# How the experts of a two-layer mixture-of-experts tower get their rows: scattered by expert, or gathered by a table from slot to token

## The reference, cut to what matters

```python
# layer 0, experts (xe: the layer-normed rows that go to expert e)
for e in range(N_EXPERTS):
    mask = (max_ind == e)[:, None]
    xe = jnp.where(mask, x, 0.0)
    oe = jax.nn.silu(xe @ w1[e]) * (xe @ w2[e]) @ w3[e]
    out = out + jnp.where(mask, oe, 0.0)
out = out.astype(jnp.bfloat16) * max_prob
# layer 1, experts
selection = scores + expert_bias[None, :]
_, top_idx = jax.lax.top_k(selection, K)             # K = 2
top_s = jnp.take_along_axis(scores, top_idx, axis=-1)
comb = jnp.zeros((T, e)).at[jnp.arange(T)[:, None], top_idx].add(top_s / (sum of top_s))
out = routed + _swiglu(xf, sg, su, sd)               # routed: sum over e of comb[:, e] * swiglu_e(xf)
```

## Time and profile before

| | us |
|---|---|
| median of 3 runs (1969.52 to 1982.78) | 1977.91 |
| the profiled execution itself | 1965.71 |
| its span | 1964.1 |
| PE busy in the span | 1599.7 (81%) |
| DVE, ACT, POOL busy | 1080.7, 619.3, 385.6 |
| mean granted TensorE clock (1 is full speed) | 0.884 |
| layer 0: last of `route` on DVE, first pair on PE | 842.64, 890.44 |
| layer 1: first shared pair, first routed pair, first pair of the tail | 1439.86, 1571.02, 1843.41 |

### The profile page before, as it was taken

The page is one execution under the profiler, slowest core; times in us unless marked ns, Lnnn a source line. Parts: engine busy times, 40 slices in busy tenths (PEclk is TensorE's granted clock), DMA queues, the critical chain, the costliest instruction groups (busy, mean ns, idle before and its releaser), DMA issues. The chain is left out here.

```text
span 1964.1 us, 28517 instructions
## 1 busy us (share of the span) xinstructions
PE 1599.7 (81%) x8996; PEld 873.7 (44%) x8997; DVE 1080.7 (55%) x2460; ACT 619.3 (32%) x840; POOL 385.6 (20%) x442
## 2 busy tenths in 40 slices
PE   5769998998999997608999479988632899999973
PEld 3412332332333325605666246677621566666642
DVE  5868996997998924612333355545620233333345
ACT  3403665665666683101111111101100122222110
POOL 6530000000000001151110460001157011111255
PEclk9856998998999998758999689997666899999987
DMA  3487222222222006011111210005012011111123
GB/s 90 126 145 223 36 33 33 33 33 33 33 33 33 1 2 187 9 59 42 40 40 36 71 28 2 2 1 166 1 50 76 7 48 52 52 52 52 50 81 91
DMA packets 86416, 106.98 MB, mean 54 GB/s; under 512 B 10481, under 2 KB 72244, under 8 KB 85300
## 3 DMA queue, kind: packets, MB, share of 16 engines
q1 hardware_dynamic: 74624, 82.39, 17.4%
q0 software_dynamic: 10752, 22.03, 3.8%
q10 hardware_dynamic: 960, 1.57, 0.5%
HBM read 61.82 MB, written 44.14 MB: 54 GB/s over the span
## 5 line engine op out<-in xcount | busy, mean ns | idle before, releaser
L510 DVE TENSOR_REDUCE sa_half_max<-psum 128x1 f32<-128x512 f32 x768 | 494.5, 687 | 65.6 <-PE psum L614 45.9
L568 ACT ACTIVATE sa_probs<-psum 128x1024 f32<-128x1024 f32 x384 | 372.6, 1022 | 169.2 <-PE psum L605 167.6
L614 PE MATMUL psum<-k_stack,q_stack 96*128 96x512 bf16 x768 | 286.8, 412 | 27.3 <-PEq L398 18.3
L605 PE MATMUL psum<-q_stack,k_stack 97*128 97x512 bf16 x768 | 232.5, 387 | 6.3 <-ACT sa_probs L568 5.4
L1191 ACT ACTIVATE ex_silu<-psum 128x384 f32<-128x384 f32 (+1 forms) x144 | 74.6, 520 | 451.4 <-PE psum L1327 334.2
L1327 PE MATMUL psum<-w_e_up_a,ex_xt 128*128 (+1 forms) x576 | 215.7, 518 | 0.0
L637 PE MATMUL psum<-sa_probs,sa_v_ext 128*32 128x512 f32 x1536 | 208.2, 614 | 0.6 <-ACT sa_probs L568 0.6
L614 PEld LDWEIGHTS psum<-k_stack,q_stack 96*128 96x128 bf16 x768 | 75.2, 98 | 284.5 <-issue 152.9
L1212 DVE TENSOR_TENSOR ex_g<-ex_silu,psum 128x384 f32<-128x384 f32 (+1 forms) x144 | 84.5, 591 | 192.0 <-PE psum L1327 165.2
L1343 PE MATMUL psum<-w_e_down,ex_g_t 128*128 (+1 forms) x944 | 177.2, 339 | 14.5 <-issue 14.2
L1343 PEld LDWEIGHTS psum<-w_e_down,ex_g_t 128*128 128x128 f32 x944 | 154.8, 193 | 60.3 <-issue 60.3
(11 more groups left out here) (229 smaller groups left out, 1854.5 us busy)
## 6 DMA issues: line engine op xcount, KB each, us to landing
ex_x<-x_rows SPq DMA_DIRECT2D x56, 192.0 KB
y_rows<-ex_y SPq DMA_DIRECT2D x56, 192.0 KB, 2.0
q_stack<-qk_parts SPq DMA_DIRECT2D x66, 128.0 KB
k_stack<-qk_parts SPq DMA_DIRECT2D x66, 128.0 KB
x_rows<-sa_zeros SPq DMA_DIRECT2D x1, 6912.0 KB
qk_parts<-ep_parts SPq DMA_DIRECT2D x16, 384.0 KB
x_rows<-sa_zeros SPq DMA_DIRECT2D x1, 3840.0 KB
qk_parts<-ep_parts SPq DMA_DIRECT2D x16, 192.0 KB
```

The costliest lines, as they stand in the source:

```text
L510: nc.vector.tensor_reduce(half_max[:, g, hd, qt, half:half + 1], slot, AX.X, ALU.max).then_inc(ring_free[r], 1)
L568: nc.scalar.activation(probs[:, st % 2, 2 * pair:2 * pair + 2, :], ps[:, 2 * pair:2 * pair + 2, :], ACT.Exp, scale=SCALE0).then_inc(exp_do ...
L605: last = nc.tensor.matmul(ps[:, hd, :], kst[:, g, hd, kt * P:(kt + 1) * P], qst[:, g, hd, half * HALF:(half + 1) * HALF], start=True, stop ...
L614: last = nc.tensor.matmul(ps[:, 4 + r, :], qst[0:SK, g, hd, qt * P:(qt + 1) * P], kst[0:SK, g, hd, half * 512:(half + 1) * 512], start=Tru ...
```

## The change

The rows of tokens are no longer scattered. `close_attention` stores each chunk of `x2` to `x_tokens` in DRAM, in the order of the tokens, from SP, whose queue has the expert weights in front of it; DVE may overwrite `x2` only when that store has landed (`s.x_saved`). `keep` stays in layer 1 alone, where the shared expert reads `attn`. `route` finds the best experts with compares and reductions over all tiles at once, and builds a table: for each tile and choice DVE makes two one-hot matrices (slot within the block, and block times token number), and PE sums their product over all tiles in PSUM, 32 matmuls in layer 0, 64 in layer 1; the sum is `s.slot_tokens`, the token of each slot (0 where there is none). In `experts` POOL gathers each routed pair's two blocks from `x_tokens` by that table, two indirect DMAs per pair, inside the loop. `LEAD` is 6 tiles, 3 pairs, so 13 pairs are in the tail. The zeros are gone with `x_rows`.

```diff
-LEAD = NT // 2
-MIXED_IN_TAIL = (1, 1, 2, 2, 2, 2, 1)
+LEAD = 6
+MIXED_IN_TAIL = (0, 1, 1, 2, 1, 2, 1, 2, 1, 2, 1, 1)
...
-            sp.wait_ge(zeroed, START + 1)
-            for x_rows, n in zip(s.x_rows, (blocks_of(1), blocks_of(2))):
-                sp.dma_start(x_rows[0:n * P, :].rearrange("(n p) d -> p n d", p=P),
-                             zeros[:].unsqueeze(1).to_broadcast([P, n, D])).then_inc(zeros_stored, 16)
-
...
+            tokens = s.x_tokens[layer].rearrange("(t p) d -> p t d", p=P)
+            with sp.Fori(0, B) as k:
+                for u in range(2):
+                    sp.wait_ge(two["x2"][u], START + k + 1)
+                    sp.dma_start(tokens[:, tiles_of((u, k)), :], x2[:, u]).then_inc(s.x_saved[u], 16)
+
...
-                if prev:
+                if prev and layer == 1:
                     keep(*prev)
 
-            pipeline(pool, B, lambda: take(0, 0), step, lambda: keep(1, B - 1))
+            def finish():
+                if layer == 1:
+                    keep(1, B - 1)
+            pipeline(pool, B, lambda: take(0, 0), step, finish)
...
-                dve.wait_ge(two["kept"][u], START + k)
+                dve.wait_ge(s.x_saved[u], START + 16 * k)
+                if layer == 1:
+                    dve.wait_ge(two["kept"][u], START + k)
                 layer_norm_apply(nc, link, tiles, x2[:, u], mv[:, u], var_eps[:, u], std[:, u],
                                  tmp[:, u]).then_inc(two["x2"][u], 1)
...
+            for i in range(KT):
+                pe.wait_ge(m["table_row"], START + 2 * (i + 1))
+                nc.tensor.matmul(ps[:, 2, 0:NBLK], in_slot[:, i % TABLE_BUFS, :], in_block[:, i % TABLE_BUFS, :],
+                                 start=(i == 0), stop=(i == KT - 1)).then_inc(m["table"], 1)
...
-            for t in range(NT):
-                last = nc.vector.max(best[:, t, :], ranked[:, t, :])
-            link(last)
-            for t in range(NT):
-                last = nc.vector.max_index(best_i[:, t, :], best[:, t, :], ranked[:, t, :])
-            link(last)
-            link(nc.vector.tensor_copy(best_f[:], best_i[:]))
...
+            for k in range(k_top):
+
+                if layer == 0:
+                    best_k = total
+                else:
+                    best_k = best
+                    link(nc.vector.tensor_reduce(best[:], ranked[:], AX.X, ALU.max))
+                link(nc.vector.tensor_tensor(tied[:], ranked[:], over(best_k[:].unsqueeze(2), te), ALU.is_equal))
+                link(nc.vector.tensor_tensor(tied[:], tied[:], over(expert_up[:].unsqueeze(1), te), ALU.mult))
+                link(nc.vector.tensor_reduce(best[:], tied[:], AX.X, ALU.min))
+                nc.vector.tensor_tensor(chosen[:, k], over(expert_up[:].unsqueeze(1), te),
+                                        over(best[:].unsqueeze(2), te), ALU.is_equal).then_inc(m["chosen"], 1)
+                dve.wait_ge(m["chosen"], START + k + 1)
+                if k + 1 < k_top:
+                    link(nc.vector.tensor_scalar(tied[:], chosen[:, k], TAKEN, None, ALU.mult))
+                    link(nc.vector.tensor_tensor(choice[:], choice[:], tied[:], ALU.add))
             link(nc.vector.tensor_copy(block_f[:], block_i[:]))
-            for k in range(k_top):
-                nc.vector.tensor_tensor(chosen[:, k], over(expert_f[:].unsqueeze(1), te),
-                                        over(best_f[:, :, k:k + 1], te), ALU.is_equal).then_inc(m["chosen"], 1)
...
+            link(nc.vector.tensor_copy(place_i[:], place_f[:]))
+            link(nc.vector.tensor_scalar(place_i[:], place_i[:], P.bit_length() - 1, None, ALU.arith_shift_right))
+            link(nc.vector.tensor_copy(place_block[:], place_i[:]))
+            link(nc.vector.tensor_scalar(place_slot[:], place_block[:], float(P), None, ALU.mult))
+            link(nc.vector.tensor_tensor(place_slot[:], place_f[:], place_slot[:], ALU.subtract))
+            for i in range(KT):
+                buf, t = i % TABLE_BUFS, i % NT
+                if i >= TABLE_BUFS:
+                    dve.wait_ge(m["table"], START + i - TABLE_BUFS + 1)
+                nc.vector.tensor_scalar(in_slot[:, buf, :], slot_f[:], place_slot[:, i:i + 1], None, ALU.is_equal
+                                        ).then_inc(m["table_row"], 1)
+                nc.vector.tensor_scalar(in_block[:, buf, :], block_f[:], place_block[:, i:i + 1], token_f[:, t:t + 1],
+                                        ALU.is_equal, ALU.mult).then_inc(m["table_row"], 1)
...
+            dve.wait_ge(m["table"], START + KT)
+            nc.vector.tensor_copy(s.slot_tokens[:, 0:NBLK], ps[:, 2, 0:NBLK])
...
-        PAIRS = LAST + FIRST
+        PAIRS = LAST + (NT // 2 - FIRST) * layer
...
-            for i in range(KT):
-                pool.indirect_dma_start(out=x_rows, out_offset=bass.IndirectOffsetOnAxis(ap=s.place[:, i:i + 1], axis=0),
-                                        in_=s.attn[:, i % NT, :], in_offset=None).then_inc(scattered[i % 8], 16)
-
-            def own_weights(k):
-
+            def own_weights(k, u):
+
+                e = pool.value_load(s.owner[0:1, bass.ds(2 * k + u, 1)], min_val=0, max_val=E - 1)
+                nc.gpsimd.tensor_copy(w_b[:, u, :], up_b[:, bass.ds(e, 1), :].rearrange("p o f -> p (o f)")
+                                      ).then_inc(w_b_done, 1)
+
+            def gather_x(k, u):
+
+                pool.indirect_dma_start(out=x[:, u, :], out_offset=None, in_=x_tokens,
+                                        in_offset=bass.IndirectOffsetOnAxis(ap=tokens[:, u:u + 1], axis=0)
+                                        ).then_inc(x_landed[u], 16)
+
+            def take_tokens(k):
+
+                nc.gpsimd.tensor_copy(tokens[:], s.slot_tokens[:, bass.ds(2 * (k - FIRST), 2)]).then_inc(tokens_taken, 1)
+                pool.wait_ge(tokens_taken, START + k - FIRST + 1)
+                pool.nop(nofuse=True)
+
+            for u in range(2):
+                pool.wait_ge(s.x_saved[u], START + 16 * B)
+            take_tokens(FIRST)
+            for u in range(2):
+                gather_x(FIRST, u)
+            pool.wait_ge(s.experts_loaded, START + 16 * s.n_expert_loads)
+            if FIRST:
+                pool.wait_ge(half_done, START + FIRST)
+            for u in range(2):
+                own_weights(FIRST, u)
+            with pool.Fori(FIRST + 1, LAST) as k:
+
+                pool.wait_ge(x_ps, START + k)
+                take_tokens(k)
+                gather_x(k, 0)
                 pool.wait_ge(half_done, START + k)
-                for u in range(2):
-                    e = pool.value_load(s.owner[0:1, bass.ds(2 * k + u, 1)], min_val=0, max_val=E - 1)
-                    nc.gpsimd.tensor_copy(w_b[:, u, :], up_b[:, bass.ds(e, 1), :].rearrange("p o f -> p (o f)")
-                                          ).then_inc(w_b_done, 1)
-            pool.wait_ge(s.experts_loaded, START + 16 * s.n_expert_loads)
-            if layer == 0:
-                own_weights(0)
-            for i in range(8):
-                pool.wait_ge(scattered[i], 16 * (KT // 8))
-            pool.nop(nofuse=True).then_inc(rows_placed, 1)
-            with pool.Fori(max(FIRST, 1), LAST) as k:
...
+                own_weights(k, 0)
+                gather_x(k, 1)
+                own_weights(k, 1)
...
-            def load(n):
-
-                if n:
-                    sp.wait_ge(x_ps, START + FIRST + n)
-                sp.dma_start(x[:], x_rows[2 * n * P:(2 * n + 2) * P, :].rearrange("(u p) d -> p u d", p=P)
-                             ).then_inc(loaded, 16)
-
             def store(n):
                 sp.wait_ge(y_done, START + FIRST + n + 1)
                 sp.dma_start(y_rows[2 * n * P:(2 * n + 2) * P, :].rearrange("(u p) d -> p u d", p=P), y[:]
                              ).then_inc(stored, 16)
 
-            sp.wait_ge(rows_placed, START + 1)
-            load(0)
-            load(1)
             for n in range(ROUTED):
-                if n + 2 < ROUTED:
-                    load(n + 2)
                 store(n)
...
-                    pe.wait_ge(loaded, START + 16 * (k - FIRST + 1))
+                    for u in range(2):
+                        pe.wait_ge(x_landed[u], 16 * (k - FIRST + 1))
```

More of the change, by code:

```diff
@@ L392, in softmax_attention @@
         out_copied = [new_sem(f"sa_out_copied{r}") for r in range(2)]
-        zeros = sb("zeros", [P, D])
-        zeroed, zeros_stored = (new_sem("sa_" + n) for n in ("zeroed", "zeros_stored"))
         inv_done, v_init, ones_row = (new_sem("sa_" + n)
@@ L483, in _ @@
             turns(sp, sequence)
-            sp.wait_ge(zeros_stored, START + 32)
         @block.gpsimd
@@ L531, in combine @@
                                         ALU.max).then_inc(max_done[g], 1)
-            nc.vector.memset(zeros[:], 0.0).then_inc(zeroed, 1)
             for n, unit in enumerate(before):
@@ L716, in close_attention, with tiles_of @@
         PS_A, PS_B, PS_O, PS_XA, PS_XB, PS_L = 0, 1, 2, 4, 5, 6
```

(35 more changed lines are left out.)

32 lines of the change are left out of this document (22 added, 10 removed).

## The result

The changed kernel takes 1896.64 us, median of 4 runs (1889.05 to 1897.78), against 1979.74 for the kernel before (4 runs, 1969.52 to 1982.78). The ratio is 0.959, 95% interval 0.956 to 0.963. The profiled execution took 1889.05, its span is 1887.3; the kernel before had 1965.71 and 1964.1, so the spans differ by 76.8 where the sum said 81.3. Later (e5, e6) both kernels were traced again.

The account below looks back on a forecast made before the run. PE bounds the routed loop; scatter waits and late PE signals hold up layer 0's start, the lead and tail. Terms sum to -81.3 us: 1884.4 against the profiled execution, 1896.6 against the median; forecast 1890, range 1850 to 1930.

Parts of the forecast that it names:

- 1.: Layer 0 before its first pair: scatters go and the pair waits only for two gathers, -39.7 us.
- 5.: Argmax in route: a few operations replace MAX8 and what follows, -5.7 us in layer 0, -2.4 in layer 1.
- 6.: Token table in route, both layers: small operations +2.1 us, PE's table matmuls +50.9, covered DVE work -2.5.
- 2.: Layer 1's lead: 64 scatters and the late PE signals go, five pairs move to the tail, -108.5 us.
- 3.: The tail with 13 pairs: half of the present time beyond PE's work comes again, +5 us (-13 to +24).
- Rival A: The longer tail is late throughout: +24 or up to +37 in place of +5, 1909 to 1922 us; chance 0.13.
- 4.: close_attention: DVE waits for x2's stores behind the weights, +10 us in layer 0, +1.5 in layer 1.
- 7.: Layer 1's routed loop: the gather for block 1 lands 0.25 us late per pair, +9 us (0 to +32).
- Rival B: Layer 1's loop: the gather for block 1 is 0.9 us late in every pair, +32, 1913 us; chance 0.12.
- 8.: The zeros' store beside a busy PE goes: -1 us.
- Rival C: Each indirect DMA beside PE costs its signals time, 1.1 us each over 112 gathers: +123, 2013 us; chance 0.07.
- rival D: The lead's stall isn't the scatters' and stays with three pairs: 70 us of gain lost, 1960; chance 0.04.

Follow-up runs that it names:

- e5: The kernel before, unchanged, traced a second time: 1967.9 us, with a lead of 130.4 us.
- e6: The changed kernel, unchanged, traced again beside runs of the kernel before: 1887.6 us, ratio 0.956 (0.951 to 0.961).
- e2b: The kernel before, scatters kept, with only LEAD = 6 and the changed kernel's list of mixes: 1911.9 us, ratio 1.003 (0.9994 to 1.0067).
- e3b: The changed kernel with LEAD back at 16 and 64 unused indirect gathers on POOL ahead of layer 1's routed loop: 1914.1 us, lead 87.2 us.
- e9: The changed kernel with SP issuing the expert weights behind the x2 stores, layer 1's expert bias loaded with the first weights: 1844.3 us, ratio 0.970.
- e7: The changed kernel with the expert weights issued from ACT's queue, x2's stores alone on SP's: 1899.2 us, ratio 0.9615 (0.956 to 0.967).
- e8: The changed kernel with empty slots pointing to 127 different rows in place of all to row 0: 1884.9 us, ratio 0.954 (0.948 to 0.961).
- e1b: The changed kernel with LEAD back at 16, 8 shared pairs ahead of the routed loop and 8 behind: 1890.5 us, ratio 0.9945 (0.9917 to 0.9973).
- e10: The changed kernel with the tail's 64 gathers held back in groups of 4 and another list of mixes: 1860.6 us, ratio 0.979 (0.9755 to 0.9825).

## Why the prediction was right, step by step

The direction, the size and the place were right. That the sum of -81.3 came so near the spans' -76.8 and -77.1 is in part luck: the tail was put 12.5 too low, and the table and the loop some 16 too high. Of the steps (after less before, means of the two pairs of traces):

1. and 5., 6. for layer 0, -28.3 predicted for route 0 and the wait, -32.2 measured. The wait for rows is as worked out. The argmax takes 840.55 to 842.76, 2.2 us against 2.3. The table is where the difference is. Up to close_attention 0 the changed kernel takes 2.9 and 4.4 us more, which no step had; some 3 of it lie in `embed_and_project`, which the change leaves alone and whose end is at 114 to 126 us over the fourteen traces.
2. The lead: -108.5, measured -108.4. But the reason holds on late chips alone. On the others the scatters with three pairs take a lead of 86 us (e2b) and 64 gathers with eight one of 87 (e3b), where the late ones have 131. How the 108.4 divide between the scatters and the moved pairs no run on a late chip shows.
3. **The tail: +5 predicted, +17.5 measured**, the largest miss, inside its range of -13 to +24. Half of the 37.7 us beyond PE's own work was assumed to go with a longer list of pairs; some 28 came again (135 to 136.5, less the 107.4 without any). Rival A was right that the lateness comes again, but its +24 or more wasn't reached. Without lateness 13 pairs take 108.7 us (e9), one more than the 107.4 worked out for that case.
4. The stores: +11.5, measured +11.9 in close_attention 0 and +0.6 in 1. Size and reason are right for this kernel: none of the store's packets starts before 789, when the first DMA engines are through with the weights in front of it, as the packets under e7 show, and it landed after 20.9 us. The rule on ring order in the Trainium skill ("DMA: Bandwidth & Descriptors", "Queues, rings and completion order") has this trace's agreement. What was wrong is the other case, that a store which shares the engines with the weights lands before it is needed: in e7 it took 24.5. The same section says that an engine takes its queues in turn, packet by packet; e7's 226 packets beside 225 agree, and turns of such unequal packets don't bring 384 KB home in time. In layer 1 DVE waited 6.6 and 2.8 us and the stage grew by 0.9 and 0.3. It isn't a good place for small differences: over all fourteen traces it takes 82 to 88 us where its granted clock is 0.71 to 0.79, and 94 to 99 where it is 0.61 to 0.66.
6. **The table: +50.9 predicted, about 40** (13.2 and 27.1 us on DVE). PE takes 0.43 us a tile in place of 0.53, which came from a row whose steps alternate between two pairs of operands and have 8 columns. That PE is the bound isn't shown: DVE's pairs are 0.41 to 0.42 apart in most steps, and DVE idles before none of them. Nor is the work on `owner` covered in layer 1. There PE ends at 1449.3, DVE's owner work at 1450.4, and the copy of the table stands behind that.
7. The loop (where POOL also copies rows 128 to 191 of each block's up weights to `ex_w_b`, which PE's L1321 reads): +9 predicted as 0.25 late in each pair; measured +3.3, nearly all of it in four pairs, and for a reason that was on no list (e8). In the other pairs the gather lands in time. Rival B's rule on two inputs in SBUF has the trace's agreement: the loop's gathers took 0.97 and 0.98 us on the median and 1.03 at most, and 1.3 came only in the tail, in the first trace seven times, each time beside a DVE operation with both inputs in SBUF.
8. The zeros: -1 predicted; from the first store of the softmax's maxima to close_attention it is 590.2 and 590.3 us. Nothing.

Rival C (each gather beside PE costs 0.7 us or more) and rival D are excluded, the first by a loop that is 3.3 us longer with 72 gathers in it, the second by leads of 22.4 and 22.2 us on chips where the kernel before has 131. D was about three pairs; whether eight without scatters would stall on such a chip wasn't run.

What the prediction could not see: the trace of before held 45 us of the lead (131 for 86) and 14 to 19 of the tail (116 to 121 for e1b's 101.7) that other chips don't have, and the changed kernel's 27 of its tail. On those, the changed kernel's worth is an estimate: its span of 1887.3, with e9's tail of 108.7 for its 136.5, is 1859.5, beside a span of some 1898 for the kernel before, so -39 us in place of -83. From e10, 1860.6 less 4.7 for its tail, beside 1901.1, it is -45.

Open: what makes PE's signals late on some chips. Shown is only where: beside POOL's indirect DMAs in the lead and the tail, never in the routed loop with two per 7.6 us. Two things differ there at once, and no run separates them: the DMAs are dense, and the pairs of lead and tail are written out one after the other, while the routed loop is one piece of code that repeats. A slow transfer of code it is not, as far as the traces show: none on the instruction queues took over 1.7 us in the traces of the two kernels. Nor can they tell whether PE's signal is late or the end of its work, since the ends of matmuls are modelled.

## What to carry to other kernels

A chain of indirect DMAs on one queue costs its number times 1.25 us (80 us for 64) before the first consumer can start; fetching rows where they are used, two per turn beside matmuls, cost this loop 3.3 us in 36 turns. A small store behind or beside megabytes of weights waited for the weights in one queue and in two; issue the weights after it, when they are needed late (e9: 72.2 us for the stage in place of 84). And a stall that one trace shows may come and go with the chip: run the kernel before in each group, and don't take a run from a chip without the stall as a verdict on its cause.

## What the runs showed of the hardware that I had not expected

- The same kernel took 1901 to 1902 us on two chips and 1970 to 1980 in the other three comparisons. In one of the slower ones DVE began 11.5 us after the PE work that it waited for the earlier trace rows, and ACT another time 37 us after it (transposes start at 1454.74, their copy at 1491.97); in e2b, on one of the two, it was 0.04.
- A gather of 128 indices that are mostly equal lands later than one of different rows: 3.45 us after its start for a block with 10 tokens and 118 repeats, and 3.82, 3.56 and 3.53 for blocks of 128 repeats, where the others took 2.5 to 2.9. PE waited 0.44, 0.82, 0.56 and 0.52 for them. With 127 different rows for the empty slots the waits were gone (e8).
- A store of 384 KB took 20.9 us in one queue with the weights, 24.5 in a queue of its own beside them, and 2.6 alone. In the first case its packets stood still, in the second they took turns one for one with packets of 18 KB.
